# Projecting K and V three tiles ahead of a sequential scan, through a DRAM place per tile

## The chip, the cores and the metric

One core of a Trainium2 chip. The metric is the device time of one execution in microseconds (us). A core has five engines that run their own instruction queues in order and wait for each other by semaphores: TensorE (PE; its weight loads are listed as PEld), VectorE (DVE), ScalarE (ACT), GpSimd (POOL) and SyncE (SP), which only issues DMAs here. ScalarE issues some DMAs too.

## The reference, cut to what matters

```python
k = x @ Wk.T; v = x @ Wv.T          # x: [2, 4096, 512], 16 heads of 32
k = k * cos + rotate_half(k) * sin
def step(W, kc, vc):                # 256 minibatches of 16 tokens, one after the other
    z = kc @ W                      # per batch and head, W starts as the 32x32 unit matrix
    return W - kc.T @ ((z - vc) * 2 / (16 * 32)), z
out = layernorm(zs) * gamma + beta
x = layernorm(x + out @ Wo.T)
h = silu((x @ gate_w.T) * gate_s) * ((x @ up_w.T) * up_s)      # 1408 wide
x = layernorm(x + (h @ down_w.T) * down_s)
```

Only `step` is sequential; K and V of every token depend on x alone.

## The kernel before, in words

The 4096 positions are cut into 32 tiles (NT) of 128 tokens, both batches together. A tile has 8 scan steps (NS). Work is written as **ticks**: tick t, from -1 to 35, has 16 slots, and every engine's program walks the same ticks and slots with its own part. In tick t the kernel projects tile t (n), scans tile t-1 (sc), does the first layernorm, the output projection and the second layernorm of tile t-2 (o), and most of the FFN of tile t-3. The first two FFN blocks of tile o (GATE_UP, DOWN and LOW give slot and block) come in slots 14 and 15.

Projection. x of the tile arrives transposed in x_fm (one buffer, load_x_fm on SyncE); ScalarE makes its high part in fm[0] (high_x, L602), VectorE the low part in fm[1] (low_x, L1076). `project` (L762) does 12 matmuls of 128x512 for one of K and V and one batch; this is called a unit here. K goes to a PSUM bank and from there by `rotate` (L989, three VectorE operations) and `add_rotated` (L481, GpSimd) to k_tok; V by `copy_v` (L583, ScalarE) to v_tok or k_sin. A usual tick has K and V of the second batch of tile t in slots 1 and 4, and those of the first batch of tile t+1 in slots 12 to 14.

K and V then go to DRAM (store_k, store_v; k_scr and v_scr hold one tile) and come back as rows per head (load_rows, 8 DMAs for each half tile of K and of V). K is also needed transposed: for tiles 0 to 2 TensorE transposes it (turn_k, L845), from tile 3 on (EARLY_TICKS) VectorE transposes 32x32 blocks into `turned` and four DMAs and one load turn the rest through kT_scr. z and x1 of tile o take the same way through zT_scr and x1T_scr (store_x1T, L376, load_x1T, L382).

Scan. An even slot has scan_z (L727): z = k W into PSUM. VectorE subtracts v (scan_err, L1012), ScalarE saves z over v_rows (save_z, L558). An odd slot has scan_state (L746), k^T err, and VectorE adds it to the state (step_state, L1022), for which the next scan_z waits. z is stored to z_scr and loaded as tokens (store_z, load_z) in three pieces; VectorE's stats_of begins the layernorm of tile o in slot 0 of the next tick.

Order of the head. The weights gate, up and down are copied DRAM to DRAM and then loaded by ScalarE's queue during ticks -1 to 2 (copy_ffn, load_ffn), and `weigh` (L1086) reduces each piece on VectorE (WEIGHED gives the slots) to find whether the FFN matmuls may run in a faster exact format. TensorE branches on that in tick 2 before slot 14, after GpSimd's all-reduce (L548). In ticks 1 and 2 the projection units are cut in quarters and halves. In the last ticks, 32 has no projection, 33 to 35 no scan.

SyncE's tick (L412) is one list of waits and issues in order: rows of the scanned tile's second half, v store, out store, z turn, x, k and v stores, z store, kT store, first z load, kT load, first-half rows, x1 turn with v rows between its store and its load, x_fm of a later tile, the rest of z.

Of the kernel before, what the change touches and what calls it, by code (L numbers as in the profile page):

```python
# [7 lines left out]
F32 = mybir.dt.float32  # L8
# [41 lines left out]
HALF_UNITS = {1: (0, 2), 2: (2, NC)}  # L50
LAST = NT - 1
LONE = 1
# [17 lines left out]
def build(nc, xT, x, wkT, wvT, woT, gamma, beta, gwT, uwT, dwT, gs, us, ds_row, rope, ident, begin, halves, out):  # L70
    with ExitStack() as ctx:
# [6 lines left out]
        k_scr = nc.dram_tensor("k_scr", [BATCH, P, DM], F32, kind="Internal").ap()  # L78
        v_scr = nc.dram_tensor("v_scr", [BATCH, P, DM], F32, kind="Internal").ap()
        z_scr = nc.dram_tensor("z_scr", [NS, P, 2, P], F32, kind="Internal").ap()  # L80
        kT_scr = nc.dram_tensor("kT_scr", [HQ, HEAD, HQ, NG, HEAD], F32, kind="Internal").ap()
# [31 lines left out]
        v_tok = [sb("v_tok", [P, DM]), k_sin]  # L113
# [18 lines left out]
        hid = [sb(f"hid{i}", [P, TOK]) for i in range(2)]  # L132
# [98 lines left out]
        def v_bank(n, b):  # L231
            return (gu_acc, down_acc[1])[b] if n == 0 else down_acc[0] if n < EARLY_TICKS else work

        def k_by_dma(n):
            return n >= EARLY_TICKS

        def kT_before(n):
            return max(0, n - EARLY_TICKS)

# [31 lines left out]
        def _(sp):  # L271
# [27 lines left out]
            def load_rows(scr, half, b):  # L299

                i0 = half * NS // 2
                for hg in range(NC):
# [4 lines left out]
                                 scr[b, i0 * MB:i0 * MB + P // 2, hg * P:(hg + 1) * P]  # L307
                                 .rearrange("(i t) c -> t i c", t=MB)).then_inc(rows_in[half], 16)

            def load_k_half0(n):  # L310
                sp.wait_ge(k_stored, 16 * (n + 1))
                if n >= 1:
                    sp.wait_ge(state_added, 4 * NS * (n - 1) + 2 * NS)
                for b in range(BATCH):
                    load_rows(k_scr, 0, b)

            def load_v_half0(n, b):
# [4 lines left out]
                load_rows(v_scr, 0, b)  # L322

            def load_k_half1(n):
                if n >= 1:
                    sp.wait_ge(state_added, 4 * NS * n)
                for b in range(BATCH):
                    load_rows(k_scr, 1, b)

            def load_v_half1(n):  # L330
                if n >= 1:
                    sp.wait_ge(z_stored, 48 * n)
                for b in range(BATCH):
                    load_rows(v_scr, 1, b)

            def store_v(n, b):
                sp.wait_ge(v_ready, 2 * n + b + 1)
                if b == 0 and n >= 1:
                    sp.wait_ge(rows_in[0], 256 * n)
                    sp.wait_ge(rows_in[1], 256 * n)  # L340
                sp.dma_start(v_scr[b], v_tok[b][:]).then_inc(v_stored, 16)
# [11 lines left out]
            def store_kT(n):  # L353
                sp.wait_ge(k_turned, 2 * n + 2)
                sp.wait_ge(kT_in, 16 * n)
                store_turned(kT_scr, kT_stored)

            def load_kT(n):
# [3 lines left out]
                             kT_scr.rearrange("h d a g t -> (h d) (a g t)")).then_inc(kT_in, 16)  # L362
# [7 lines left out]
            def load_znT(n):  # L370
                sp.wait_ge(znT_stored, 64 * zT_before(n + 1))
                sp.wait_ge(x1_lo_ready, 2 * n)
                sp.dma_start(landed[:].rearrange("p a g t -> p (a g t)"),
# [14 lines left out]
            def load_x(n):  # L388
                if n == 0:
                    sp.wait_ge(w_low, 2 * NC)  # L390
# [21 lines left out]
            def tick(t):  # L412
                sc, o, y = t - 1, t - 2, t - 4
                if within(sc) and sc >= 1:
                    load_k_half1(sc)
                if within(sc) and sc >= 1:
                    load_v_half1(sc)
                if within(t):
                    store_v(t, 0)
                if y == LAST:  # L420
                    for b in range(BATCH):
                        sp.wait_ge(y_ready, 2 * y + b + 1)
                        sp.dma_start(out[b, rows(y), :], y_tok[:, b, :]).then_inc(out_stored, 16)
                elif within(y):
                    sp.wait_ge(y_ready, 2 * y + 2)
                    sp.dma_start(out[:, rows(y), :].rearrange("b t f -> t b f"), y_tok[:]).then_inc(out_stored, 16)
                if within(o) and z_by_dma(o):
                    store_znT(o)
                    load_znT(o)
                if within(o):  # L430
                    load_x(o)
                if within(t):
                    store_k(t)
                    store_v(t, 1)
                if t == 0:
                    load_k_half0(t)
                    load_k_half1(t)
                if within(sc):
                    store_z(sc, 0, NS // 2)
                if within(t) and k_by_dma(t):  # L440
                    store_kT(t)
                if within(sc):
                    load_z(sc, 0, NS // 2, 16)
                if within(t) and k_by_dma(t):
                    load_kT(t)
                if within(t) and t >= 1:
                    load_k_half0(t)
                if within(o) and z_by_dma(o):
                    store_x1T(o)
                if within(t) and t >= 2:  # L450
                    load_v_half0(t, 0)
                if within(o) and z_by_dma(o):
                    load_x1T(o)
                if within(t) and t >= 2:
# [771 lines left out]
```

## Time and profile before

| | us |
|---|---|
| runs, median of 3 | 1939.27 (1938.07 to 1940.27) |
| profiled execution, device time | 1946.0 |
| its span, first to last instruction | 1944.2 |
| TensorE busy | 1852.8 (95%), 25792 matmuls |
| VectorE busy | 1186.0 (61%) |
| ScalarE busy | 547.9 (28%) |
| GpSimd busy | 638.4 (33%) |
| mean granted TensorE clock | 0.983 |

A busy share is taken over the whole span. The rows further down are of single stretches. A timeline row has start, duration, engine, line, operation, output and inputs, the count of merged instructions and, in brackets, the idle time before it and what ended it. Matmuls overlap in the pipeline, so their price is the distance from start to start. A tick's start is that of the scan_z (L740) of its slot 0.

### The profile page before, as it was taken

What the parts mean: (1) busy time and instruction counts of PE and PEld (TensorE: products, weight loads), DVE (VectorE), ACT (ScalarE), POOL (GpSimd) and SP (SyncE); (2) the same over time, 40 slices, a digit from 0 to 9 for tenths busy, and PEclk for the clock granted to TensorE, in tenths of its full rate; (3) what the DMA queues carried; (4) which work ended last, traced back from release to release, by engine and by line L of the source; (5) the groups of instructions that cost most, each with busy time, mean ns of one, the idle gap of its engine ahead of it and who ended that gap; (6) DMA issues with size and microseconds to landing.
All of it is one profiled execution on the core that took longest, in us unless ns stands there. A gap on an engine that the chain in (4) does not pass through costs nothing.

```text
span 1944.2 us, 60610 instructions
## 1 busy us (share of the span) xinstructions
PE 1852.8 (95%) x25792; PEld 1478.3 (76%) x25792; DVE 1186.0 (61%) x2612; ACT 547.9 (28%) x1236; POOL 638.4 (33%) x775
## 2 busy tenths in 40 slices
PE   6569999999999999999999999999999999999887
PEld 4348777877877777877777787777878878777676
DVE  3555666666666656666665666666666666666643
ACT  2113222232223232322223232222322232322222
POOL 1113333333333333333333333333333333333333
PEclk9779999999999999999999999999999999999999
DMA  7674554455444455545445545444554544555310
GB/s 265 201 222 134 152 151 129 140 166 165 140 147 147 141 146 162 157 144 155 127 144 161 164 143 159 148 130 141 165 167 139 151 147 137 148 153 150 93 55 23
DMA packets 302512, 287.26 MB, mean 148 GB/s; under 512 B 42784, under 2 KB 252320, under 8 KB 302112
## 3 DMA queue, kind: packets, MB, share of 16 engines
q1 hardware_dynamic: 295968, 265.26, 46.0%
q10 hardware_dynamic: 6272, 18.09, 2.7%
q8 instruction: 205, 3.36, 0.7%
q14 instruction: 67, 0.55, 0.1%
HBM read 152.65 MB, written 139.20 MB: 150 GB/s over the span
## 4 chain that ended last, share of the span: by engine, by line
PE 76%; DVE 9%; DMA 7%; SPq 4%; ACT 2%; issue 2%; ACTq 0%; POOL 0%; POOLq 0%; DVEq 0%
PE gu_acc L787 30%; PE work L768 24%; PE down_acc L799 13%; PE scan_acc L740 4%; PE scan_acc L757 3%; DVE x_tok L956 2%; SPq L306 2%; DMA z_scr<-v_rows 2%; DVE hid L1032 2%; DMA landed<-x1T_scr 2%; DVE turned L961 2%; DVE state L1027 1%; DMA landed<-zT_scr 1%; SPq L350 1%; ACT hid L571 1%
## 5 line engine op out<-in xcount | busy, mean ns | idle before, releaser
L500 POOL TENSOR_TENSOR hid_lo<-hid,hid_hi 128x256 fp32r<-128x256 f32 x352 | 263.0, 747 | 629.9 <-ACT hid_hi L581 629.8
L787 PE MATMUL gu_acc<-x_hi,gw 128*128 128x256 f32 x1372 | 375.2, 306 | 8.7 <-DVE hid L1032 3.2
L571 ACT ACTIVATE hid<-gu_acc,gate_scale 128x256 f32<-128x256 f32 x343 | 162.6, 474 | 765.6 <-PE gu_acc L787 765.4
L1032 DVE SCALAR_TENSOR_TENSOR hid<-gu_acc,up_scale,hid 128x256 f32<-128x256 f32 x343 | 165.5, 483 | 300.5 <-ACT hid L571 300.5
L787 PE MATMUL gu_acc<-x_lo,gw 128*128 128x256 f32 x1372 | 339.5, 280 | 0.0
L787 PE MATMUL gu_acc<-x_hi,uw 128*128 128x256 f32 x1372 | 338.8, 280 | 0.0
L787 PE MATMUL gu_acc<-x_lo,uw 128*128 128x256 f32 x1372 | 338.0, 279 | 0.0
L1027 DVE SCALAR_TENSOR_TENSOR state<-scan_acc,half_step,state 128x256 f32<-128x256 f32 x512 | 223.5, 478 | 170.2 <-PE scan_acc L757 164.9
L787 PEld LDWEIGHTS gu_acc<-x_hi,gw 128*128 128x128 f32 x1372 | 258.0, 188 | 44.9 <-DVE hid L1032 18.7
L799 PE MATMUL down_acc<-dw,hid_hi 128*128 128x512 f32 x704 | 282.0, 401 | 2.4 <-POOL hid_lo L500 2.2
L799 PE MATMUL down_acc<-dw,hid_lo 128*128 128x512 f32 x704 | 279.1, 396 | 0.0
L787 PEld LDWEIGHTS gu_acc<-x_lo,gw 128*128 128x128 f32 x1372 | 259.0, 189 | 0.4
L787 PEld LDWEIGHTS gu_acc<-x_hi,uw 128*128 128x128 f32 x1372 | 258.2, 188 | 0.0
L787 PEld LDWEIGHTS gu_acc<-x_lo,uw 128*128 128x128 f32 x1372 | 258.0, 188 | 0.0
L768 PE MATMUL work<-wk,fm 128*128 128x512 f32 x756 | 202.9, 417 | 11.1 <-DVE fm L1078 11.1
L768 PE MATMUL work<-wo,fm 128*128 128x512 f32 x768 | 196.6, 405 | 7.8 <-DVE x_tok L1074 4.5
L581 ACT ACTIVATE hid_hi<-hid 128x256 fp32r<-128x256 f32 x352 | 146.9, 417 | 139.7 <-DVE hid L1032 138.4
L768 PE MATMUL work<-wv,fm 128*128 128x512 f32 x696 | 180.1, 401 | 4.2 <-DVE k_sin L1009 4.2
L560 ACT ACTIVATE v_rows<-scan_acc 128x256 f32<-128x256 f32 x256 | 97.6, 381 | 292.6 <-DVE err L1017 283.2
L768 PEld LDWEIGHTS work<-wk,fm 128*128 128x128 f32 x756 | 141.4, 195 | 47.3 <-DVE fm L1078 11.5
L768 PEld LDWEIGHTS work<-wo,fm 128*128 128x128 f32 x768 | 141.0, 190 | 41.1 <-issue 5.0
L740 PEld LDWEIGHTS scan_acc<-state,k_cols 64*32 64x32 f32 x8192 | 75.9, 107 | 124.2 <-issue 97.8
(121 smaller groups left out, 2230.4 us busy)
## 6 DMA issues: line engine op xcount, KB each, us to landing
x_fm<-xT SPq DMA_DIRECT2D x64, 256.0 KB, 3.4
k_scr<-k_tok SPq DMA_DIRECT2D x32, 512.0 KB, 6.6
k_rows<-k_scr SPq DMA_DIRECT2D x512, 32.0 KB, 2.1
z_scr<-v_rows SPq DMA_DIRECT2D x32, 512.0 KB, 3.5
z_tok<-z_scr SPq DMA_DIRECT2D x512, 32.0 KB, 1.8
x_tok<-x SPq DMA_DIRECT2D x32, 512.0 KB, 5.7
out<-x_tok SPq DMA_DIRECT2D x31, 512.0 KB, 3.4
v_rows<-v_scr SPq DMA_DIRECT2D x488, 32.0 KB, 2.0
```

What stands on the lines that cost most here:

```text
L306: sp.dma_start(place[:, i0:i0 + NS // 2, :], scr[b, i0 * MB:i0 * MB + P // 2, hg * P:(hg + 1) * P] .rearrange("(i t) c -> t i c", t=MB)).t ...
L500: pool.tensor_tensor(hid_lo[m % RING][:], hid[m % 2][:], hid_hi[m % RING][:].bitcast(F32), ALU.subtract).then_inc(hid_lo_ready, 1)
L560: act.activation(v_rows[:, i].rearrange("p a (r c) -> p a r c", r=2), z_acc.rearrange("p r (a c) -> p a r c", a=2), ACT.Copy).then_inc(z_s ...
L571: act.activation(hid[m % 2][:], gu_bank(n, m)[:, 0:TOK], ACT.Silu, scale=gate_scale[:, m:m + 1]).then_inc(silu_done, 1)
L581: act.activation(hid_hi[m % RING][:], hid[m % 2][:], ACT.Copy).then_inc(hid_hi_ready, 1)
L740: mm = pe.matmul(z_acc[j * HEAD:(j + 1) * HEAD, r, odd * 2 * HEAD:(odd + 1) * 2 * HEAD], lhsT=k_cols[k, i // 2, g, i % 2, :], rhs=state[k, ...
L757: mm = pe.matmul(step_acc[q, j, :], lhsT=k_rows[k, i, q], rhs=err[k, :, h, :], start=True, stop=True, skip_group_check=True, tile_position ...
L768: mm = pe.matmul(acc[:], lhsT=fm[p_x][:, c, b, :], rhs=w[p_w][:, c, :], start=(c == 0 and k == 0), stop=(c == NC - 1 and k == 2))
L787: mm = pe.matmul(gu_bank(n, m)[:, k * TOK:(k + 1) * TOK], lhsT=w[:, c, m * P:(m + 1) * P].bitcast(dt), rhs=part[:, c].bitcast(dt), start=( ...
L799: mm = pe.matmul(down_acc[b][:], lhsT=part[m % RING][:, b * P:(b + 1) * P].bitcast(dt), rhs=dw[:, m, :].bitcast(dt), start=(m == 0 and par ...
L1027: dve.scalar_tensor_tensor(part, step_acc.rearrange("p j (o e) -> p j o e", o=2), half_step[:, e:e + 1], part, ALU.mult, ALU.add).then_inc ...
L1032: dve.scalar_tensor_tensor(hid[m % 2][:], gu_bank(n, m)[:, TOK:2 * TOK], up_scale[:, m:m + 1], hid[m % 2][:], ALU.mult, ALU.mult).then_inc ...
```

## The change

K and V of a tile are projected three ticks earlier (LEAD): in a usual tick t the units are those of tile t+3, and of t+4 in slots 12 to 14. k_scr, v_scr and kT_scr get one place per tile, so that stores wait for no load. Tick 1 has a half unit in each of its 16 slots (8 units) and four whole units behind slot 15; tick 2 has six units in slots 0 to 5 and two more in halves in slots 9, 10, 12 and 13. Ticks 29 to 31 have no units left, tick 28 none in slots 12 to 14. Staging for odd tiles up to 5 is lent by v_tok, hid and landed, for even ones v uses x_tok. K of tiles 0 and 1 is transposed on TensorE, from tile 2 on by DMA. In ticks 1 and 2 low_x is on GpSimd, the scaling of wo on ScalarE, and the FFN weights are copied, loaded and weighed in other slots; v rows of tile 1 are loaded by SyncE.

```diff
-WEIGHED = {(1, 13): (0,), (1, 15): (1,), (2, 1): (2,), (2, 3): (3,), (2, 6): (4,), (2, 8): (5,), (2, 10): (6,), (2, 11): (7,),
-           (2, 12): (8,), (2, 13): (9, 10, 11)}
-EARLY_TICKS = 3
+WEIGHED = {(1, 5): (0,), (1, 8): (1,), (1, 11): (2,), (1, 13): (3,), (2, 0): (4,), (2, 2): (5,), (2, 4): (6,), (2, 6): (7,),
+           (2, 9): (8,), (2, 10): (9,), (2, 11): (10,), (2, 13): (11,)}
+STEADY = 3
+LEAD = 3
+FRONT = STEADY + LEAD
+BY_PE = 2
+HALVES = ((0, 2), (2, NC))
+FIRST_UNITS = ((K, 1, 1), (V, 1, 1), (K, 2, 0), (V, 2, 0), (K, 2, 1), (V, 2, 1), (K, 3, 0), (V, 3, 0))
+MIDDLE_UNITS = ((K, 3, 1), (V, 3, 1), (K, 4, 0), (V, 4, 0))
+SECOND_UNITS = ((K, 4, 1), (V, 4, 1), (K, 5, 0), (V, 5, 0), (K, 5, 1), (V, 5, 1))
...
-        k_scr = nc.dram_tensor("k_scr", [BATCH, P, DM], F32, kind="Internal").ap()
+        k_scr = nc.dram_tensor("k_scr", [NT, BATCH, P, DM], F32, kind="Internal").ap()
...
+        def k_half(n, b):
+            if n < FRONT and n % 2:
+                return v_tok[:] if b == 0 else hid_both[:].rearrange("p a t -> p (a t)")
+            return k_tok[:, b, :]
+        def v_half(n, b):
+            if n == 0 or n >= FRONT:
+                return (v_tok, k_sin)[b][:]
+            if n % 2:
+                return landed[:].rearrange("p h g t -> p (h g t)")[:, b * DM:(b + 1) * DM]
+            return x_tok[:, b, :]
...
             def store_k(n):
-                sp.wait_ge(k_ready, 2 * n + 2)
-                sp.dma_start(k_scr.rearrange("b t f -> t b f"), k_tok[:]).then_inc(k_stored, 16)
+                sp.wait_ge(k_stored, 32 * n)
+                for b in range(BATCH):
+                    sp.wait_ge(k_ready, 2 * n + b + 1)
+                    sp.dma_start(k_scr[n, b], k_half(n, b)).then_inc(k_stored, 16)
...
             def load_x(n):
                 if n == 0:
-                    sp.wait_ge(w_low, 2 * NC)
+                    sp.wait_ge(v_stored, 32 * (FRONT - 1))
...
+                elif t == 1:
+                    store_v(1, 0)
+                    store_k(1)
+                    store_v(1, 1)
+                    load_x_fm(3)
+                    store_z(0, 0, NS // 2)
+                    load_k_half0(1)
+                    load_z(0, 0, NS // 2, 16)
+                    store_v(2, 0)
+                    load_v_half0(1, 0)
+                    load_v_half0(1, 1)
+                    store_k(2)
+                    store_z(0, NS // 2, NS - 1)
+                    store_v(2, 1)
+                    load_x_fm(4)
+                    load_z(0, NS // 2, NS - 1, 32)
+                    store_kT(2)
+                    store_z(0, NS - 1, NS)
+                    load_z(0, NS - 1, NS, 48)
+                elif t == 2:
+                    load_k_half1(1)
+                    load_v_half1(1)
+                    store_v(3, 0)
+                    store_k(3)
+                    store_v(3, 1)
+                    load_x_fm(5)
+                    store_v(4, 0)
+                    store_kT(3)
+                    store_k(4)
+                    store_v(4, 1)
+                    load_kT(2)
+                    load_x_fm(6)
+                    load_x(0)
+                    store_v(5, 0)
+                    store_kT(4)
+                    store_k(5)
+                    store_z(1, 0, NS // 2)
+                    store_v(5, 1)
+                    load_k_half0(2)
+                    load_z(1, 0, NS // 2, 16)
+                    store_kT(5)
+                    load_v_half0(2, 0)
+                    load_v_half0(2, 1)
+                    load_x_fm(7)
...
+                else:
...
+                    if within(n):
+                        store_v(n, 0)
...
+                    if within(t):
+                        load_kT(t)
+                        load_k_half0(t)
...
+            def low_x(n, b):
+                pool.wait_ge(x_high, 2 * n + b + 1)
+                pool.tensor_tensor(fm[1][:, :, b, :], x_fm[:, :, b, :], fm[0][:, :, b, :].bitcast(F32),
+                                   ALU.subtract).then_inc(x_low, 1)
...
-                if within(o + 2):
-                    pe.wait_ge(v_ready, 2 * (o + 2) + 2)
+                if o == 0:
+                    pe.wait_ge(k_mul, 6 * FRONT)
+                elif within(o + 2 + LEAD):
+                    pe.wait_ge(v_ready, 2 * (o + 2 + LEAD) + 2)
...
+                    if t == 1:
+                        unit(*FIRST_UNITS[s // 2], *HALVES[s % 2])
+                    if t == 1 and s == 15:
+                        for middle in MIDDLE_UNITS:
+                            unit(*middle, 0, NC)
+                    if t == 2 and s < len(SECOND_UNITS):
+                        unit(*SECOND_UNITS[s], 0, NC)
+                    if t >= STEADY and within(n) and s == 1:
+                        project_k(n, 1, 0, NC)
+                    if t >= STEADY and within(n) and s == 4:
+                        project_v(n, 1, 0, NC)
...
+                    if t == 2 and s in (9, 10):
+                        project_k(FRONT, 0, *HALVES[s - 9])
+                    if t == 2 and s in (12, 13):
+                        project_v(FRONT, 0, *HALVES[s - 12])
...
-                    if within(o) and s == (0 if o != LAST else 3):
+                    if within(o) and s == (2 if o == 0 else 3 if o == LAST else 0):
                         dve.wait_ge(z_tok_in, 256 * (o + 1))
                         stats_of(0, 0, z_tok)
```

## Rows read from the trace of the kernel before

**Rows 1.** Windows: busy time per engine in stretches: ticks 1, 2, a usual one, 31, 32.

```profile
core 0: us, PE busy (x) PEld busy (x) DVE busy (x) ACT busy (x) POOL busy (x), PEclk, DMA share, GB/s
34.30:73.40 39.10, 26.89 (x573) 15.83 (x572) 20.40 (x42) 8.24 (x18) 4.17 (x7) 0.83 0.72 231
73.40:150.10 76.70, 43.63 (x645) 31.89 (x644) 39.42 (x68) 11.66 (x23) 9.16 (x12) 0.76 0.63 199
1523.90:1580.90 57.00, 56.80 (x805) 45.51 (x804) 36.46 (x82) 16.77 (x38) 20.14 (x25) 1.00 0.50 150
1752.90:1808.80 55.90, 52.51 (x781) 42.31 (x780) 33.92 (x77) 15.24 (x35) 19.20 (x24) 0.97 0.49 143
1808.80:1861.50 52.70, 45.96 (x758) 36.89 (x757) 31.50 (x72) 14.68 (x35) 16.71 (x21) 1.00 0.33 99
```

**Rows 2.** Timeline of TensorE, ticks 1 and 2: the large gaps.

```profile
70.13 0.47 PE L757 MATMUL scan_acc<-err,k_rows 32*32 32x64 f32 x16 [4.33 <-ACT v_rows L560]
...
90.25 0.68 PE L740 MATMUL scan_acc<-state,k_cols 64*32 64x64 f32 x32 [9.96 <-DVE state L1027]
...
112.55 5.37 PE L768 MATMUL work<-wo,fm 128*128 128x512 f32 x12 [3.54 <-DVE x_tok L1074]
...
141.38 0.68 PE L740 MATMUL scan_acc<-state,k_cols 64*32 64x64 f32 x32 [7.53 <-issue]
```

**Rows 3.** Waits of the head, and what VectorE and GpSimd do before the branch.

```profile
ACT v_rows L560 <- issue: 9.5, 1, 9.5
DVE stats L942 <- DMA z_tok<-z_scr: 11.1, 1, 11.1
...
132.05 1.74 DVE L1089 TENSOR_REDUCE low_half<-dw 128x1 f32<-128x1536 uint16 x1
...
132.21 1.29 POOL L484 TENSOR_TENSOR k_tok<-k_tok,k_sin 128x512 f32<-128x512 f32 x1 [10.60 <-DVE k_sin L1009]
...
139.65 0.17 DVE L1182 TENSOR_REDUCE low_half<-low_half 128x1 f32<-128x12 f32 x1
```

**Rows 4.** Timeline of TensorE: one unit in a usual tick, and what follows it.

```profile
1527.68 3.06 PE L768 MATMUL work<-wk,fm 128*128 128x512 f32 x12
1530.67 0.45 PE L740 MATMUL scan_acc<-state,k_cols 64*32 64x64 f32 x32
```

**Rows 5.** Timeline of TensorE, ticks 31 and 32: slot 12, and a gap of each.

```profile
1795.38 0.45 PE L740 MATMUL scan_acc<-state,k_cols 64*32 64x64 f32 x32
...
1800.90 0.68 PE L740 MATMUL scan_acc<-state,k_cols 64*32 64x64 f32 x32 [2.49 <-DVE state L1027]
...
1814.89 0.46 PE L740 MATMUL scan_acc<-state,k_cols 64*32 64x64 f32 x32 [2.28 <-DVE state L1027]
...
1850.49 0.46 PE L740 MATMUL scan_acc<-state,k_cols 64*32 64x64 f32 x32
```

**Rows 6.** Timeline of SyncE: the x1 turn in tick 31 and in tick 32.

```profile
1789.61 1.75 SPq L350 DMA_DIRECT2D x1T_scr<-turned  x4
...
1794.84 0.34 SPq L385 DMA_DIRECT2D landed<-x1T_scr  x1
...
1844.72 1.76 SPq L350 DMA_DIRECT2D x1T_scr<-turned  x4
...
1848.38 0.34 SPq L385 DMA_DIRECT2D landed<-x1T_scr  x1
```

**Rows 7.** DMA of 34.3 to 150.1: bytes, queues' share of 16 engines, us to landing.

```profile
DMA packets 19338, 24.25 MB, mean 209 GB/s; under 512 B 2652, under 2 KB 14142, under 8 KB 19262
...
q10 hardware_dynamic: 5539, 14.96, 38.8%
q1 hardware_dynamic: 13787, 9.12, 26.8%
...
x_fm<-xT SPq DMA_DIRECT2D x6, 256.0 KB, 3.7
...
k_scr<-k_tok SPq DMA_DIRECT2D x2, 512.0 KB, 7.4
```

More of the change, by code:

```diff
@@ L130, in build @@
         x1_lo = sb("x1_lo", [P, NC, BATCH, P], F32R)
-        hid = [sb(f"hid{i}", [P, TOK]) for i in range(2)]
+        hid_both = sb("hid", [P, 2, TOK])
+        hid = [hid_both[:, i, :] for i in range(2)]
         hid_hi = [sb(f"hid_hi{i}", [P, TOK], F32R) for i in range(RING)]
@@ L412, in tick @@
             def tick(t):
[L413 to L454, printed above, removed]
-                    load_v_half0(t, 1)
@@ L691, in tick @@
                             copy_ffn(0, c)
-                    if within(t) and not k_by_dma(t) and s == (9 if t == LONE else 6):
+                    if within(t) and not k_by_dma(t) and s == (7 if t == 1 else 6):
                         copy_kT(t, 0)
@@ L698, in tick @@
                         act.wait_ge(small_in, 16 * SMALL)
+                    if t == 1 and s in (1, 3, 5, 7):
+                        scale_wo(s // 2)
                     if t == 1 and s in (2, 4, 6, 8):
@@ L1124, in tick @@
                         normalize(1, o, 1, x1_tok[o % 2], x_tok, x1_ready)
-                    if within(t + 1) and s == 11:
+                    if t <= 0 and s == 11:
                         low_x(t + 1, 1)
+                    if t >= STEADY - 1 and within(n + 1) and s == 11:
+                        low_x(n + 1, 1)
                     if within(o) and s == (12 if o != LAST else 10):
@@ L1146, in tick @@
                         moments_of(0, o)
-                    if within(o) and s == (1 if o != LAST else 4):
+                    if within(o) and s == (3 if o == 0 else 4 if o == LAST else 1):
                         normalize(0, o, 0, z_tok, z_tok, zn_ready)
@@ L1156, in tick @@
                         turn_x1(o, 1)
-                    if within(t) and s == (5 if t == LONE else 2):
-                        rotate(t, 1)
-                    if within(o) and s == (5 if o != LAST else 6):
+                    if t == 0 and s == 2:
+                        rotate(0, 1)
+                    if t >= STEADY and within(n) and s == 2:
+                        rotate(n, 1)
+                    if within(o) and s == (6 if o in (0, LAST) else 5):
                         low_zn(o, 1)
-                    if within(t + 1) and s == 7:
+                    if t <= 0 and s == 7:
                         low_x(t + 1, 0)
+                    if t == 2 and s == 8:
+                        low_x(FRONT, 0)
+                    if t >= STEADY and within(n + 1) and s == 7:
+                        low_x(n + 1, 0)
                     if t == -1 and s == 12:
```

449 lines of the change are left out of this document (314 added, 135 removed).

## The prediction, made before the changed kernel was seen to run

> **What bounds the kernel now.** I read the stretches first [rows 1]. In a usual tick (1523.9 to 1580.9) TensorE is busy 56.80 of 57.00 us at the full clock, so nothing but its own work sets the tick. Three places are different. Ticks 1 and 2 last 39.1 and 76.7 us and hold 26.9 and 43.6 us of TensorE work, part of it at half clock (granted 0.83 and 0.76). Tick 31 (55.9 us) lacks the first batch's projections of a next tile, and tick 32 (52.7 us) has none. So the kernel has room at the head and loses cover at the tail; the change moves TensorE work from the tail ticks to the head.
>
> Then the TensorE rows of the head [rows 2]. A TensorE row in brackets is a gap with its releaser. Tick 1 runs from 34.3 to 73.4, tick 2 to 150.1. Large gaps: 4.33 us before 70.13 (ScalarE saved z late: it stood 9.5 us in its own issues [rows 3], the eight row loads of load_v_rows among them), 9.96 before 90.25, 3.54 before 112.55, 7.53 before 141.38. The 9.96 is VectorE standing 11.1 us for z_tok's DMA [rows 3], with step_state behind it in the same queue. The 7.53 is the end of weigh: the last reduction ends at 139.8, GpSimd's all-reduce follows, then TensorE branches [rows 3]. A scan step's two matmul groups are priced at 0.7 us together below, their rows of 0.45 and 0.47 [rows 2, 4] less the overlap.
>
> Last the TensorE rows of ticks 31 and 32, and SyncE's for the x1 turn [rows 5, 6].
>
> **The size of what moves.** One unit (12 matmuls, one of K/V, one batch) takes 1530.67 - 1527.68 = 2.99 us from start to start [rows 4]; four per tile. After the change ticks 1 and 2 hold 20 units (8 + 4 middle, then 6 + 2) instead of 8: 12 more, 12 x 2.99 = 35.9 us. They leave tick 28 (two), ticks 29 and 30 (four each) and tick 31 (two). The time changes only by what the head stretches and the tail shrinks.
>
> **The tail.** Tick 32 already is a tick with scan and FFN and no unit. It lost 4 x 2.99 = 12.0 us of work against a usual tick but only 57.0 - 52.7 = 4.3 us of time [rows 1]: TensorE idles 52.7 - 46.0 = 6.7 us in it, the longest gap 2.28 us, for state [rows 5]. These are scan latencies that the units had covered, and the next thing late is step_state behind other VectorE work. By halves: slots 0 to 11 take 1850.5 - 1808.8 = 41.7 us against 1795.4 - 1752.9 = 42.5 in tick 31, which has its two units there: 0.8 back of 6.0. Slots 12 to 15 take 1861.5 - 1850.5 = 11.0, against 1808.8 - 1795.4 = 13.4 in tick 31 and 57.0 - 42.5 = 14.5 in a usual one.
> The two ends of slots 12 to 15 differ through one wait. In tick 31 SyncE issues the x1T load 5.23 us after its stores began, in tick 32 3.66 [rows 6]; four v_rows loads of the next tile stand between. With the load late, ScalarE's x_hi and VectorE's x_lo are late, step_state waits behind x_lo, TensorE idles 2.49 us.
> Worst: all four shortened ticks end in 13.4: tick 28 gives 1.1, 29 and 30 give 57.0 - 55.1 = 1.9 each, 31 gives 55.9 - 55.1 = 0.8; together 5.7 us. Best: all end in 11.0: 3.5 + 4.3 + 4.3 + 3.2 = 15.3 us. Four stores issue in 1.75 us, so four loads as quick would be through after 3.5 and fit before the 3.66 at which tick 32 issues: the 5.23 of tick 31 is more than its queue explains, and I stand nearer to tick 32: 10 us gained. In ticks 29 to 31 SyncE also loses store_k, store_v, store_kT and x_fm; no queue gets anything more.
>
> **The usual ticks, 3 to 27.** TensorE's order is the same. store_k becomes two DMAs (one more issue on SyncE), kT and rows are loaded for a tile stored three ticks before, so load_kT and the k and v row loads wait for no landing. The rotate and copy waits keep their form, shifted. All of it lies under 56.8 of 57.0 us of TensorE work: 0. If that cover were gone, the extra issue would cost some 0.4 us a tick (one issue takes 0.34 to 0.44 [rows 6]), 10 us in all. Bounds: the 25 ticks have 0.2 us of idle each [rows 1], so at most 5 us to win, more likely none, and a hiccup in two or three of them to lose: -3 to +3 us.
>
> **The head.** Tick 1: a scan step with a half unit after each part is 0.7 + 2 x 1.5 = 3.7 us of TensorE work. Before, with quarter units, the tick took 39.1 us, 4.33 of them that gap: 34.8 us or 4.3 a step, more than TensorE's work: latency of err, save and state. I take 35 us again, then four middle units, 12 us, of which none covers a scan; start of tick 2 at 34 + 47 = 81 to 82, against 73.4. The wait for ScalarE's issue (4.33) and most of the 9.96 go: load_v_rows(1) moves to SyncE, and stats of z_tok move from slot 0 to 2, behind two to four units.
> What the units need: x_fm has one buffer. Tile n+1 is loaded only when both low halves of tile n are made, lands 3.7 us later [rows 7] or more, then ScalarE and GpSimd do one 128x512 operation each, 1.3 us each at most (GpSimd's add [rows 3]); that is up to 6.3 us after low_x(n, 1), and units K and V of (n, 1) fill 6.0. Just enough, if SyncE comes to it in time and the DMA is quick. The queue ahead on SyncE in tick 2 is 16 row loads (16 x 0.44 = 7 us), two v stores and k: I allow 3 us of stalls in tick 2.
> Also moved: low_x of tiles 2 to 5 goes from VectorE to GpSimd, 8 x 1.3 = 10 us on an engine busy 13.3 of 115.8 us [rows 1]; scale_wo goes from VectorE to ScalarE (19.9 us busy in 115.8 [rows 1]); both free VectorE and lie beside TensorE's units.
> Tick 2: slots 0 to 5, 3 x (0.7 + 6.0) = 20 us; 3 of stalls; two project_o with their turn and the wait for add_o (x is loaded only after v of tile 4 is stored, because x_tok is its staging; it was 3.5 us late before and stays so), 10 us; slots 8 to 13 with two units in halves, turn_x1, four weigh of up to 1.74 us [rows 3] and K rotation on VectorE, 20 us; slots 14 and 15 as before, 150.1 - 141.4 = 8.7. Sum 62, against 76.7. Tick 3 begins at 82 + 62 = 144 to 145; before 150.1. Gain 5 us.
> Bounds. DMA: in this stretch 24.25 MB took 66% of 16 engines for 115.8 us, that is 316 GB/s when busy [rows 7]. The change adds three tiles each of x, k and v, four kT stores and one kT load, 14 x 0.524 = 7.3 MB. 31.6 MB at 316 GB/s are 100 us: best, a gain of 16. At tick 1's mean, 231 GB/s [rows 1], 137 us: a loss of 21.
> The page "DMA: Bandwidth & Descriptors" (Bandwidth) of the Trainium skill gives about 358 GB/s as a core's HBM limit; by it the bytes alone would take an estimated 88 us. No run here shows that rate over such a stretch, and the sum does not use it.
>
> **Sum.** Profiled execution 1946.0 us: -5 (head), 0, -10 (tail) = 1931.0. It lies 6.7 us above the median of the runs, 1939.27; so 1924.3.
>
> **Rivals.**
> (a) The head fills without stalls, as fast as the bytes allow, and the tail ends well: -16 - 13 = -29, 1910 us. For: TensorE had 45 us free there. Against: k lands after a median of 7.4 us in the head [rows 7], and x_fm may come to that too. Chance 0.12.
> (b) The head eats the tail's gain: FFN copies, row loads and three more tiles share 16 DMA engines, and SyncE serves x_fm behind waits for k_ready and for landing z. Head +8 to +13: within 0.2%. Chance 0.10.
> (c) The same at 231 GB/s: +21 - 10 = +11, 1950 us. It decides from the point where ticks 1 and 2 together pass 126 us. For: the bytes grow by 30%, and the queue is one and in order. Against: the DMA engines idle a third of the time now. Chance 0.10.
> (d) TensorE's clock. The thinned ticks 28 to 32 have gaps; after the 2.49 us gap of tick 31 the granted clock is 0.97 over it, and in the head, with gaps, 0.76 to 0.83 [rows 1]. If ticks 29 to 32 ran at the head's 0.76, 46 us of work would take 60 and each tick some 8 us more than my 53.5: +32 - 15 = +17, 1956 us. Against: tick 32 itself has 6 us of gaps and granted 1.00. Chance 0.03. The page "TensorE: Matmul & The Clock Gate" (HAM oscillation) says that bursts shorter than the waits between them let the clock fall before each burst, so that each begins at half. By this case's rows that holds in the head and not in tick 32, whose bursts are longer than its gaps.
> (e) That it doesn't do what it says can be left out: units, places and waits are written out in the diff.
>
> **How the numbers follow.** Forecast 0.65, (a) 0.12, (b) 0.10, (c) 0.10, (d) 0.03. A measurement here can tell about 0.2%, 3.9 us. Faster: 0.77, same 0.10, slower 0.13. The forecast alone spans head -12 to +2, tail -15 to -6 and up to 3 from the usual ticks, 1909 to 1935; the range with the inner parts of (a), (b) and the near end of (c) is 1908 to 1941.
>
> **What would show it.** Tick 2 begins near 82 and tick 3 near 145; the 4.33 and 9.96 gaps are gone, the 7.53 is smaller; DMA share of the head is over 0.8. Usual ticks stay 57.0. Ticks 29 to 31 take 52.7 to 55.1, with gaps before z, err and project_o as in tick 32. Wrong if tick 3 begins after 160, if x_fm or z_tok is what TensorE or VectorE waits for there by over 10 us, or if ticks 29 to 31 run at half clock.

## The result, and the profile after

| | before | after |
|---|---|---|
| median of the runs, us | 1938.67 (1934.59 to 1940.27) | 1956.11 (1949.63 to 1958.09) |
| ratio, 95% interval | | 1.0087 (1.0062 to 1.0111) |
| profiled execution, us | 1946.0 | 1949.63 |
| its span, us | 1944.2 | 1947.5 |
| TensorE busy, us | 1852.8 | 1856.3 |

The change makes the kernel slower by 17 us; the forecast was 15 us faster. The profiled execution is the shortest of the changed kernel's four. Windows of the changed kernel, cut at its tick starts: ticks 1, 2, 3, then 28 to 31. They stand beside [rows 1].

```profile
core 0: us, PE busy (x) PEld busy (x) DVE busy (x) ACT busy (x) POOL busy (x), PEclk, DMA share, GB/s
33.40:92.40 59.00, 48.63 (x665) 34.04 (x664) 29.22 (x52) 15.62 (x30) 17.06 (x17) 0.91 0.89 293
92.40:165.50 73.10, 51.84 (x689) 38.74 (x688) 41.85 (x77) 12.76 (x25) 15.02 (x17) 0.81 0.63 197
165.50:222.50 57.00, 56.59 (x804) 45.34 (x804) 35.41 (x79) 16.69 (x38) 19.47 (x23) 1.00 0.48 140
1594.20:1650.40 56.20, 52.93 (x786) 42.67 (x786) 33.83 (x77) 15.36 (x35) 19.14 (x24) 0.97 0.49 143
1650.40:1705.40 55.00, 48.48 (x757) 39.55 (x756) 31.34 (x72) 14.63 (x34) 17.23 (x23) 0.94 0.39 116
1705.40:1759.10 53.70, 45.96 (x758) 36.94 (x757) 31.25 (x72) 14.64 (x34) 17.43 (x23) 1.00 0.39 117
1759.10:1814.20 55.10, 48.85 (x761) 39.94 (x761) 31.11 (x72) 14.75 (x34) 17.48 (x23) 0.94 0.40 119
```

The head is the loss: tick 3 begins at 165.5, not at 144.5 (before: 150.1). The usual ticks are as they were: ticks 3 to 27 take 1428.7 us, before 1430.8. The tail gains: ticks 28 to 31 take 220.0 us against 227.9 for ticks 28 to 31 before. Note the 0.94 in ticks 29 and 31, and that tick 30 at 1.00 is the shortest.

TensorE's timeline of the changed kernel's head, the large gaps:

```profile
84.19 5.49 PE L955 MATMUL work<-wk,fm 128*128 128x512 f32 x12 [6.63 <-POOL fm L560]
...
108.82 5.16 PE L955 MATMUL work<-wk,fm 128*128 128x512 f32 x12 [9.26 <-POOL fm L560]
...
130.53 4.58 PE L955 MATMUL work<-wo,fm 128*128 128x512 f32 x12 [2.00 <-DVE x_tok L1281]
...
155.22 0.68 PE L927 MATMUL scan_acc<-state,k_cols 64*32 64x64 f32 x32 [3.01 <-issue]
```

The 4.33 and 9.96 of [rows 2] are gone and the 7.53 became 3.01, as forecast. In their place stand two new ones, before K of tile 4 and before K of tile 5: GpSimd's low part of x is not there. The waits of ticks 1 and 2 give the next link, ScalarE, and what it waits for:

```profile
engine line waited for: us in total, times, longest us
POOL fm L560 <- ACT fm L730: 45.6, 6, 14.7
...
ACT fm L730 <- DMA x_fm<-xT: 26.5, 4, 12.8
```

So it is x_fm's DMA. SyncE's timeline says why that is late:

```profile
69.44 3.86 SPq L325 DMA_DIRECT2D v_rows<-v_scr  x8
73.40 0.86 SPq L365 DMA_DIRECT2D k_scr<-k_tok  x2
...
75.59 2.14 SPq L295 DMA_DIRECT2D x_fm<-xT  x2
...
84.14 0.73 SPq L307 DMA_DIRECT2D z_scr<-v_rows  x1
90.55 0.77 SPq L316 DMA_DIRECT2D z_tok<-z_scr  x2
91.36 3.71 SPq L325 DMA_DIRECT2D k_rows<-k_scr  x8
95.11 5.12 SPq L325 DMA_DIRECT2D v_rows<-v_scr  x8
...
102.22 1.36 SPq L295 DMA_DIRECT2D x_fm<-xT  x2
```

x_fm was free for tile 4 at 67.1 (low_x(3, 1) ends) and its load is issued at 75.59, 8.5 us late, behind row loads and stores. It was free for tile 5 at 86.6 and the load is issued at 102.22, 15.6 us late: SyncE stands from 84.9 to 90.5 for the landing of a z store, then issues 16 row loads in 9 us, then four stores. From the issue, tile 4's x takes 6.6 us and tile 5's 4.6 us until ScalarE can begin, and 2.0 us more until K's matmuls start. And the loads take longer to land. The DMA view of 33.4 to 165.5, against [rows 7]:

```profile
DMA packets 27084, 31.70 MB, mean 240 GB/s; under 512 B 3661, under 2 KB 20221, under 8 KB 27005
...
x_fm<-xT SPq DMA_DIRECT2D x12, 256.0 KB, 5.1
```

The bytes are the 31.6 MB forecast; x_fm lands after a median of 5.1 us, before 3.7; in the second profile of each kernel it is 4.3 against 3.9. The page "DMA: Bandwidth & Descriptors" (Latency and other measured facts) of the Trainium skill says that HBM's access latency grows under load; the trace agrees in kind, at a DMA share of 0.89 in tick 1 (before: 0.72), but it does not tell latency of the memory from time spent behind other transfers.

Last, the tail. TensorE's timeline around the start of tick 29 in the changed kernel, and a window behind the second gap:

```profile
1641.98 0.46 PE L927 MATMUL scan_acc<-state,k_cols 64*32 64x64 f32 x32 [2.24 <-DVE state L1234]
...
1656.44 0.68 PE L927 MATMUL scan_acc<-state,k_cols 64*32 64x64 f32 x32 [2.28 <-DVE state L1234]
```

```profile
core 0: us, PE busy (x) PEld busy (x) DVE busy (x) ACT busy (x) POOL busy (x), PEclk, DMA share, GB/s
1656.30:1659.70 3.40, 3.25 (x44) 3.09 (x45) 3.37 (x8) 0.00 (x0) 0.97 (x3) 0.50 0.12 42
```

Each thinned tick has such gaps near slots 1 and 13, and most of them are followed by a stretch at 0.50, 1.2 GHz. From tick 28 to 1830 these add up to 20 us at half clock, in the kernel before to 3.4 us. They vary from execution to execution: again, the second profile of the changed kernel, has 34 us there, and before_again, a second one of the kernel before, 6.8.

### The profile page after: what moved, and what is told of

It reads as the page before. It is cut to its first block, busy times and chain, and to the rows that moved or that the text cites. A ratio compares the mean times of both kernels' runs of the same rounds, so it can differ in the third digit from the quotient of the medians.

```text
span 1947.5 us, 60662 instructions
## 1 busy us (share of the span) xinstructions
PE 1856.3 (95%) x25784; PEld 1483.4 (76%) x25784; DVE 1182.8 (61%) x2602; ACT 550.9 (28%) x1238; POOL 653.3 (34%) x783
## 3 DMA queue, kind: packets, MB, share of 16 engines
q8 instruction: 204, 3.34, 0.7%
## 4 chain that ended last, share of the span: by engine, by line
PE 78%; DVE 10%; DMA 5%; SPq 3%; ACT 2%; issue 1%; ACTq 0%; POOL 0%; POOLq 0%; DVEq 0%
PE gu_acc L974 32%; PE work L955 24%; PE down_acc L988 13%; PE scan_acc L927 4%; PE scan_acc L944 4%; DMA landed<-x1T_scr 2%; DVE x_tok L1154 2%; DVE state L1234 2%; DVE hid L1239 2%; DVE turned L1159 2%; SPq L325 1%; SPq L370 1%; DMA z_scr<-v_rows 1%; ACT hid L687 1%; PE scan_acc L974 1%
## 5 line engine op out<-in xcount | busy, mean ns | idle before, releaser
L974 PE MATMUL gu_acc<-x_hi,gw 128*128 128x256 f32 x1372 | 379.5, 309 | 11.5 <-DVE hid L1239 5.5
L974 PE MATMUL gu_acc<-x_lo,gw 128*128 128x256 f32 x1372 | 343.6, 283 | 0.0
L697 ACT ACTIVATE hid_hi<-hid 128x256 fp32r<-128x256 f32 x352 | 146.9, 417 | 138.9 <-DVE hid L1239 137.1
L955 PE MATMUL work<-wv,fm 128*128 128x512 f32 x624 | 162.5, 403 | 2.3 <-DVE k_sin L1216 2.0
L927 PEld LDWEIGHTS scan_acc<-state,k_cols 64*32 64x32 f32 x8192 | 75.7, 107 | 116.4 <-issue 92.1
```

The lines of the kernel that those rows point to most:

```text
L697: act.activation(hid_hi[m % RING][:], hid[m % 2], ACT.Copy).then_inc(hid_hi_ready, 1)
L927: mm = pe.matmul(z_acc[j * HEAD:(j + 1) * HEAD, r, odd * 2 * HEAD:(odd + 1) * 2 * HEAD], lhsT=k_cols[k, i // 2, g, i % 2, :], rhs=state[k, ...
L955: mm = pe.matmul(acc[:], lhsT=fm[p_x][:, c, b, :], rhs=w[p_w][:, c, :], start=(c == 0 and k == 0), stop=(c == NC - 1 and k == 2))
L974: mm = pe.matmul(gu_bank(n, m)[:, k * TOK:(k + 1) * TOK], lhsT=w[:, c, m * P:(m + 1) * P].bitcast(dt), rhs=part[:, c].bitcast(dt), start=( ...
```

## The experiments

Ratios are to the kernel before in the same job, with their 95% interval; 0.1% is 1.9 us. Where only the profiled execution is named, it is one execution.

**Again.** The changed kernel, unedited.

> The changed kernel once more, unedited, beside the others of this job; its further profile also tells what differs between executions. Both theories: 1950 to 1958 us, tick 2 begins near 92, tick 3 near 165 us, TensorE waits twice for the low half of x (6 to 9 us each) in front of K of tile 4 and K of tile 5.

1955.37 us, 1.0078 (1.0050 to 1.0105); profiled 1955.37, tick 3 at 167.7. The loss repeats, as expected. The average of the two ratios, 1.0082, is what the edits below are read against.

**The queue.** x_early issues x_fm of tiles 4 and 5 earlier on SyncE:

```diff
                     store_v(2, 0)
+                    load_x_fm(4)
                     load_v_half0(1, 0)
...
                     store_v(2, 1)
-                    load_x_fm(4)
...
                     store_z(0, NS - 1, NS)
+                    load_x_fm(5)
                     load_z(0, NS - 1, NS, 48)
...
                     store_v(3, 1)
-                    load_x_fm(5)
```

> Theory Q (SyncE's order): the loads of x_fm for tiles 4 and 5 were issued 8.5 and 15.6 us after their low halves were free, behind row loads, stores and the landing of z. Issued ahead of these, both TensorE gaps (6.6 and 9.3 us) go, tick 3 begins at 146 to 151 and the time falls by 13 to 19 us, to about 1939. Theory D (bytes): 16 DMA engines are 0.89 busy in tick 1, so an earlier issue lands later and delays the rest; tick 3 begins at 160 or later, the time falls by less than 5 us.

1949.70 us, 1.0051 (1.0031 to 1.0071); tick 3 at 157.1. TensorE's gaps in the head of x_early:

```profile
80.28 4.62 PE L955 MATMUL work<-wk,fm 128*128 128x512 f32 x12 [2.54 <-POOL fm L560]
...
106.06 5.46 PE L955 MATMUL work<-wk,fm 128*128 128x512 f32 x12 [4.60 <-DVE k_sin L1216]
```

That lies between the two theories: tick 3 is 10.7 us earlier than the average of the changed head (below), the time falls by about 6 us. 6.63 became 2.54, and where 9.26 stood the releaser is another: VectorE's rotation of K of tile 5. Its output goes to the place from which store_k(3) still reads, and SyncE's timeline of x_early has that store behind the row loads:

```profile
90.46 3.97 SPq L325 DMA_DIRECT2D k_rows<-k_scr  x8
94.47 4.71 SPq L325 DMA_DIRECT2D v_rows<-v_scr  x8
99.28 0.37 SPq L359 DMA_DIRECT2D v_scr<-landed  x1
...
100.18 0.56 SPq L365 DMA_DIRECT2D k_scr<-hid  x1
```

So queue2 also takes the stores of tile 3 ahead of those 16 loads:

```diff
-                    load_x_fm(5)
+                    store_v(3, 0)
+                    load_x_fm(5)
+                    store_k(3)
+                    store_v(3, 1)
                     load_z(0, NS - 1, NS, 48)
                 elif t == 2:
                     load_k_half1(1)
                     load_v_half1(1)
-                    store_v(3, 0)
-                    store_k(3)
-                    store_v(3, 1)
```

> As x_early, and SyncE also stores k and v of tile 3 before the 16 row loads of tick 2, since rotate of tile 5 waited for that store there (gap of 4.6 us in x_early). Theory Q: that gap goes and tick 3 begins 4 to 6 us earlier than the 157.1 of x_early, at 151 to 153: no earlier than before the change (150.2), because four units behind slot 15 (12 us) lie beside no scan step. Time 3 to 6 us under x_early's. If the bytes bound it, the gap moves to another load and tick 3 stays at 156 or later.

1944.71 us, 1.0031 (1.0018 to 1.0044); tick 3 at 155.5. The order of one queue is worth 0.5%, 10 us, with the same instructions and bytes. The time fell as forecast, but tick 3 did not come at 151 to 153. One gap is left in tick 2 of queue2, 4.89 us for the same GpSimd row: x_fm of tile 5, free at 84.0 and issued at 88.38 here, still comes behind a z store, and it lands only after 8.6 us.

**The bytes.** thin leaves out 9 of the 12 copies of the FFN weights from DRAM to DRAM; all pieces are loaded from the first one's place, so the weights in the FFN are not the reference's.

```diff
             def copy_ffn(i, c):
+                if c > 0:
+                    return
...
-                act.wait_ge(ffn_copied[i][c], 16)
-                act.dma_start(dst[:, c0:c1].bitcast(F32), src[c0 * P:c1 * P].rearrange("(c p) n -> p c n", p=P)
+                act.wait_ge(ffn_copied[i][0], 16)
+                act.dma_start(dst[:, c0:c1].bitcast(F32), src[0:(c1 - c0) * P].rearrange("(c p) n -> p c n", p=P)
```

> Of gate, up and down only the first piece is copied in DRAM and every piece is loaded from it, so 9 of 12 copies (6.3 MB) are left out and the FFN's weights are other ones. Theory Q: x_fm of tile 5 still stands behind 16 row loads and two landings; at most a third of the gaps goes, the time falls by 2 to 7 us. Theory D: with 20% fewer bytes in ticks 1 and 2 the gaps go, the time falls by 12 us or more.

1947.50 us, 1.0039 (1.0021 to 1.0057); tick 3 at 156.2. Windows of ticks 1 and 2 of thin, its bytes over both, and its largest gap:

```profile
core 0: us, PE busy (x) PEld busy (x) DVE busy (x) ACT busy (x) POOL busy (x), PEclk, DMA share, GB/s
34.40:83.40 49.00, 44.38 (x665) 31.12 (x664) 29.03 (x52) 15.40 (x30) 17.10 (x16) 1.00 0.87 273
83.40:156.20 72.80, 51.61 (x685) 38.59 (x684) 41.74 (x77) 12.63 (x25) 15.05 (x17) 0.81 0.63 191
```

```profile
DMA packets 25428, 27.24 MB, mean 224 GB/s; under 512 B 3470, under 2 KB 19637, under 8 KB 25397
```

```profile
99.86 5.03 PE L957 MATMUL work<-wk,fm 128*128 128x512 f32 x12 [9.28 <-POOL fm L560]
```

With 4.5 MB less (14%, not the 20% expected), the time again falls between the two theories. Tick 1 is 10 us shorter, and part of that is the clock, 1.00 in place of 0.91: the gap of 6.63 is 2.13 there. Tick 2 is as long as with the bytes, and the gap for tile 5 is the same 9.28: here its load was issued 13.1 us after x_fm was free, so that one is the queue's. queue2_thin has both edits:

> queue2 with 9 of the 12 DRAM copies of the FFN weights left out (the FFN's weights are other ones), for theory D with the queue out of the way. If bytes now hold the rest of the head, landings fall from 5 to 8 us to 3 to 5 us, tick 3 begins at 148 or earlier and the time is 6 us or more under queue2's 1944.7. If not, tick 3 stays at 152 to 155.

1938.81 us, 0.9987 (0.9971 to 1.0004); tick 3 at 148.9. The copies' bytes are worth 0.43 to 0.44%, 8 us, with either order. Even so tick 3 begins no earlier than before the change. The landings did not fall as expected: x_fm of tile 5 still takes 8.7 us, with a gap of 4.61 us behind it. Two things stay open. thin also takes the copies' issues, some 0.5 us each, off ScalarE's queue; and no run leaves the copies out of the kernel before, so the 8 us are what these bytes are worth in the changed head, not shown to be what the change's own 7.3 MB cost.

**A shorter lead.** lead2 projects two tiles ahead: 16 units in ticks 1 and 2, no middle units, one tile less of x, k and v in the head.

```diff
-LEAD = 3
+LEAD = 2
...
-MIDDLE_UNITS = ((K, 3, 1), (V, 3, 1), (K, 4, 0), (V, 4, 0))
-SECOND_UNITS = ((K, 4, 1), (V, 4, 1), (K, 5, 0), (V, 5, 0), (K, 5, 1), (V, 5, 1))
+SECOND_UNITS = ((K, 3, 1), (V, 3, 1), (K, 4, 0), (V, 4, 0), (K, 4, 1), (V, 4, 1))
...
-                    if within(o) and s == 4:
+                    if within(o) and s == (6 if o == 0 else 4):
                         add_bias(o, 0)
```

> K and V two tiles ahead instead of three: no units behind slot 15 of tick 1, tick 2 has the units of tiles 3 and 4, x_fm of tile 4 is loaded early. Theory Q with the cover argument: the head sheds 12 us of TensorE work that no scan step covered and both gaps, tick 3 begins at 133 to 140; the tail has three thinned ticks instead of four and gives 2 to 3 us less. 1925 to 1935 us, faster than before the change. Theory D: tick 3 begins at 150 or later.

1952.75 us, 1.0072 (1.0045 to 1.0099); tick 2 at 75.7, tick 3 at 171.9. TensorE's gaps in tick 2 of lead2:

```profile
85.04 0.79 PE L928 MATMUL scan_acc<-err,k_rows 32*32 32x64 f32 x32 [5.90 <-DVE err L1205]
...
106.33 0.68 PE L911 MATMUL scan_acc<-state,k_cols 64*32 64x64 f32 x32 [9.38 <-DVE state L1215]
...
135.30 5.23 PE L939 MATMUL work<-wo,fm 128*128 128x512 f32 x12 [14.40 <-DVE x_tok L1262]
```

A miss. Tick 2 takes 96.2 us. The middle units had covered z's round trip through DRAM; without them step_state stands behind z_tok again, as before the change (9.96 in [rows 2]). The 14.40 is x: x_tok is the staging of V of tile 4, now projected late, and x is loaded at 129.10. This run moves the wait and does not price the lead itself.

**The x1 turn.** tail_x1 lets no row load stand between the x1T stores and the load, from tick 28 on.

```diff
-                    if within(t):
+                    if within(t) and t < NT - LEAD - 1:
                         load_v_half0(t, 0)
                     if within(o) and z_by_dma(o):
                         load_x1T(o)
+                    if within(t) and t >= NT - LEAD - 1:
+                        load_v_half0(t, 0)
```

> From tick 28 on SyncE issues the x1T load ahead of all eight v row loads instead of behind four. If the gap of 1.8 to 2.6 us near slot 13 in ticks 28 to 31 is the late x1T load, it becomes the 0.6 to 1.0 of tick 32 and each of the four ticks is 1.3 to 2.4 us shorter, with the half-clock stretch after it gone: 6 to 8 us in all. If it is VectorE's own order, nothing changes (within 2 us).

1952.18 us, 1.0067 (1.0045 to 1.0089): not told apart from the changed kernel. SyncE's timeline of tick 29, in tail_x1:

```profile
1690.57 3.29 SPq L370 DMA_DIRECT2D x1T_scr<-turned  x4
1695.64 0.34 SPq L406 DMA_DIRECT2D landed<-x1T_scr  x1
```

5.07 us, with four loads less between; the changed kernel has 5.24 there (1686.00 and 1691.24). In tail_x1 nothing is issued between the end of the stores' issue (1693.86) and the load, and a store of this turn lands after a median of 3.0 us. The load waits for the stores to land, not for its place in the queue.

**The clock.** warm fills the short gaps of the thinned ticks with work that nobody reads: eight matmuls of 128x512 before the waits in slots 1 and 13 of ticks 28 to 32 (28: slot 13 alone).

```diff
+            def keep_warm(o):
+                pe.wait_ge(o_added, 2 * o)
+                for i in range(2 * NC):
+                    pe.matmul(work[:], lhsT=wo[0][:, i // 2, 0:P], rhs=wk[0][:, i // 2, :], start=(i == 0), stop=(i == 2 * NC - 1))
...
+                    if NT - LEAD <= t <= NT and s == 1:
+                        keep_warm(o)
+                    if NT - LEAD - 1 <= t <= NT and s == 13:
+                        keep_warm(o + 1)
```

> Eight extra matmuls of 128x512 into a free bank (1.7 us) in slots 1 and 13 of ticks 28 to 32, where TensorE idled 2.3 to 2.6 us; their result is not used. Theory C (clock): these gaps bring the half-clock stretches of the thinned ticks (31 to 50 us in the tail against 16 before the change), and a stretch costs half its length. With the gaps filled the half-clock time from tick 28 on falls to 16 us or less and the time by 5 to 12 us although work was added; runs differ less from each other. If the gaps themselves are the whole price, the time stays within 2 us or rises.

1946.74 us, 1.0046 (1.0025 to 1.0066). Windows of ticks 29 to 31 of warm:

```profile
core 0: us, PE busy (x) PEld busy (x) DVE busy (x) ACT busy (x) POOL busy (x), PEclk, DMA share, GB/s
1650.00:1702.70 52.70, 49.91 (x778) 39.88 (x778) 30.43 (x72) 14.65 (x34) 17.05 (x23) 1.00 0.41 122
1702.70:1754.90 52.20, 49.79 (x776) 39.84 (x776) 31.24 (x72) 14.64 (x34) 17.42 (x23) 1.00 0.41 122
1754.90:1807.00 52.10, 49.75 (x776) 39.85 (x776) 30.35 (x72) 14.65 (x34) 17.17 (x23) 1.00 0.41 124
```

Here TensorE does more work and the ticks are shorter: 157.0 us in all, 163.8 in the changed kernel. The longest gap from 1590 to 1810 is 0.76 us and no stretch there runs at half clock. The starts of scan_z give the price of one stretch: from slot 2 to slot 4 a step takes 6.99 us in all three ticks of warm and in tick 30 of the changed kernel, and 8.15 and 8.25 in its ticks 29 and 31, which have half clock there; from slot 14 to the next tick 6.79 to 6.86 against 8.06 and 8.38. That is 1.2 to 1.5 us for each stretch, and six stretches of the changed kernel's tail 7 to 9 us. Tick 30 has none; its 53.7 against 52.2 lies in slots 6 and 7, where the output projection waited 1.73 us for the low part of z, whose turn through zT_scr landed late. The run's ratio says 0.36%, 7 us. The same fill in the kernel before (ticks 31 and 32 alone) is before_warm, the control:

> The kernel before the change, with the eight extra matmuls in slot 13 of tick 31 and slots 1 and 13 of tick 32, where it too idles. It tells how much of warm's gain the kernel before could have had as well. Theory C: it has two thinned ticks instead of five and 16 us at half clock in its tail, so 1 to 4 us under the kernel before, against the 9 us that warm gained.

1939.40 us, 0.9991 (0.9974 to 1.0009): not told apart from nothing, though the interval does not exclude the 1 to 4 us expected, and from tick 28 to the end its profile has 359.8 us against 362.8 in three profiles without the fill. Most of the loss to the clock belongs to the thinned ticks that the change adds. lead2 with the fill:

> lead2 with the extra matmuls of warm (in its thinned ticks). Theory C: 3 to 8 us under lead2, 1920 to 1930 us. Otherwise within 2 us of lead2 or above it.

1948.40 us, 1.0052 (1.0032 to 1.0072), 0.2% from lead2, within the intervals of both. Its one profile agrees with theory C all the same: from tick 28 to the end it takes 352.1 us, lead2's 358.6.

**Queue and clock together.** queue2_warm is queue2 with the fill of warm.

> Both repairs at once. If the two causes are separate, their gains of 11 us (queue2) and 9 us (warm) add up: 1935 to 1937 us, 2 to 4 us under the kernel before the change; tick 3 begins at 155, ticks 28 to 31 take 52 to 55 us each, half clock in the tail about 10 us. If they share a cause, 1940 us or more.

1936.96 us, 0.9979 (0.9963 to 0.9995): this one is faster than both kernels, by 4 us against the one before. Against before_warm, the kernel before with the same fill, it is 2.4 us, which the intervals do not tell from nothing. Tick 3 begins at 161.6 here, not at the 155 expected, with queue2's order of the head: from one execution to the next this head moves by 6 us. The two profiles average 158.5, 9 us ahead of the changed kernel's. queue3_warm issues x_fm(5) ahead of kT and of the last z store too:

```diff
+                    load_x_fm(5)
                     store_kT(2)
                     store_z(0, NS - 1, NS)
                     store_v(3, 0)
-                    load_x_fm(5)
                     store_k(3)
```

> As queue2_warm, and x_fm of tile 5 is issued before the stores of kT and of the last z piece, about 3 us earlier. Theory Q: the gap of 4.9 us before K of tile 5 shrinks to about 2 and the time falls by 2 to 3 us, to 1932 to 1935 us. If its slow landing (6.8 to 8.1 us against a median of 3.5 in the whole run) is what counts, less than 1.5 us.

1938.26 us, 0.9992 (0.9976 to 1.0009); not told apart from queue2_warm. x_fm of tile 5 was issued 2.9 us after it was free and no gap of TensorE above 2 us waits for it any more, but others have grown: the output projection waits 5.61 us for x_tok, in queue2_warm 3.34. Moving this load further ahead gave nothing more.

**The kernel before, again.** before_again and before_third are the kernel before, unedited, for where its tick 3 begins.

> The kernel before the change, unedited. Its first profile has tick 3 at 150.2 us in an execution of 1946.0, 7 us above its median. If its head varies with the landings of the weights and of z, tick 3 begins at 143 to 147 in an execution near 1939 and the ticks from 3 on take the same; then the change cost the head about 20 us, not 15. If the 7 us lie elsewhere, tick 3 stays at 150.

> The same once more, for the spread of its head and its tail from execution to execution: tick 3 between 143 and 151, ticks 28 to 31 within 226 to 228 us together.

before_again: 1943.01 us, 1.0010 (0.9993 to 1.0027), its own scatter; before_third: one execution, 1944.65. Ticks 28 to 31 take 226.6 and 227.4 us. Tick 3 begins at 147.0 and 146.2. With before_warm's 144.3 the four profiles of this head average 146.9, and the 150.2 of [rows 2] is the latest of them. The four profiles with the changed head (the changed kernel, again, tail_x1, warm) have 165.5, 167.7, 170.0 and 167.9, on average 167.8. The head costs 20.9 us, not the 15.4 that the two first profiles show.

## Why the prediction was wrong, point by point

**Where the forecast failed** is one term: "I allow 3 us of stalls in tick 2", and with it the clause "Just enough, if SyncE comes to it in time and the DMA is quick". Neither held. The chain from low_x(n, 1) to the next unit was costed at 6.3 us with x_fm's load issued at once; it was issued 8.5 and 15.6 us late. I had counted 16 row loads, two v stores and k as 7 us of queue, but not as a delay that x_fm sees in full, nor the wait for the landing z store ahead of them, and had allowed no stall for tile 4, in the middle units, at all. Measured from the end of low_x(n, 1) to K's first matmul, the chain took 17.1 us for tile 4 (8.5 until the issue, 6.6 until ScalarE began, 2.0 of preparation) and 22.2 us for tile 5 (15.6, 4.6 and 2.0). By stages: slots 0 to 15 of tick 1 took 38.4 us (forecast 35), the middle units 20.6 (12), slots 0 to 5 of tick 2 32.4 (23 with the stalls), the rest 40.7 (38.7). Two of the four terms miss by 8.6 and 9.4 us, and they hold the two gaps of 6.63 and 9.26, each with a stretch at half clock behind it (a unit of 5.49 and 5.16 us in place of 3.06). The other two miss by 3.4 and 2.0, which no run takes apart.

**The sum** has the head at +20.9 us by four profiles each, ticks 3 to 27 at 1428.5 against 1431.1 (-2.6), and from tick 28 to the end 355.1 (two profiles) against 362.8 (three): -7.7. That is +10.6, of the 15 to 17 us between the medians. The other 5 or 6 stay open: unprofiled executions of the kernel before are on average some 5 us shorter than its three profiled ones, and those of the changed kernel are not.

**The usual ticks**: 0 forecast, -2.6 measured, within the bounds. **The tail**: 10 us gained forecast, about 8 measured, so right in size, but in part by luck, for its reading was off. "The 5.23 of tick 31 is more than its queue explains" was a misreading: I gave the four loads the 1.75 us of four stores, and the trace of the kernel before has 3.12 for them, so that the issues fill the 5.23 but for 0.4:

```profile
1791.47 3.12 SPq L306 DMA_DIRECT2D v_rows<-v_scr  x4
```

Yet I let the x1 turn decide between the ends, and tail_x1 shows that it does not hang on the loads between: without them the landing of the stores takes as long. What kept the gain down is the clock, as warm shows: with the fill the same stretch takes 344.9 us, 10 less than without.

**Rival (c)**, given 0.10, is the one whose sign came: ticks 1 and 2 took 132.1 us together, past its point of 126, and the head's +21 is its price. Its reason is only a part of it. A mean rate is a result of how full the queue is kept: 240 GB/s with all the bytes, 224 with 4.5 MB less, and in tick 1 of x_early, below, 317 over 53 us, as high as the 316 that the prediction took as its best.

```profile
34.60:87.60 53.00, 46.28 (x665) 32.42 (x664) 29.23 (x52) 15.50 (x30) 17.06 (x17) 0.97 0.94 317
```

The runs give the order of the queue 10 us and the bytes of nine copies 8; what the change's own bytes cost is not shown apart.

**Rival (d)**, given 0.03, was too lightly set aside. That its 1956 us is the median measured is luck: it reached it by 32 us of clock in the tail. I priced it as whole ticks at 0.76 and argued against it that tick 32 has gaps and granted 1.00. It comes as short stretches behind single gaps of 2.2 to 2.6 us, at 0.94 to 0.97 for a tick, and costs 7 us, 10 from queue2. The tick 31 of [rows 1] already had it: one gap of 2.49 us and 0.97. The page "TensorE: Matmul & The Clock Gate" (HAM oscillation) of the Trainium skill has the clock fall over waits longer than the bursts between them; here it falls over waits far shorter than the bursts too: 2.24 us before 1641.98 and 2.28 before 1656.44, with 12 us of work between the two.

**The parts together.** Queue 0.5%, bytes 0.4% and clock 0.4% are 1.3% by three single edits, against a loss of 0.8%: without all three the change would give about 0.5%, 9 us, by this estimate. Part of that may not be the change's: a kernel before without the copies was not run, and leaving them out is no repair. All three together were not run either; two pairs were, and they add up within the intervals (queue2_warm 0.9979 against 0.9995 by the sum, queue2_thin 0.9987 against 0.9988). The forecast's idea, units moved beside an idle engine, was lost to what feeds them and to the clock of what they leave behind.

## What to carry to other kernels

When work is moved into a stage to fill an idle engine, write out the in-order queue that feeds it, issue by issue, and ask of each load when its buffer comes free and what is issued or waited for in between; with one buffer, a late issue becomes the engine's gap as soon as the work in hand is used up. Price bytes and landing time at the load of the fuller stage, not at the average of the emptier one. And work that is taken away to shorten a stage leaves gaps: a gap of two microseconds cost 1.2 to 1.5 more in clock here, so look at the granted clock of the stage that already looks as the others will.

## What the runs showed of the hardware

Eight unused matmuls, twice a tick, make a tick shorter: 16 of them add 3.8 us of busy time (49.8 against 45.96 in tick 30 of the changed kernel, which is at full clock too), all of it inside the gaps, and ticks 29 to 31 shrink by 6.8 us together, most of it because the clock stays at 2.4 GHz. In the kernel before the same gaps, two in ticks 31 and 32, cost nothing that the ratio can tell. Whether a given gap is followed by a half-clock stretch is not fixed: the 2.28 us gap early in tick 32 of the kernel before kept 1.00 in [rows 1], and the same tick of before_again, its last row below, has 0.93.

```profile
1749.20:1805.00 55.80, 52.77 (x788) 42.49 (x791) 32.94 (x77) 15.22 (x35) 18.71 (x24) 0.97 0.48 144
1805.00:1857.50 52.50, 46.61 (x745) 38.06 (x745) 29.59 (x66) 14.14 (x33) 15.79 (x20) 0.93 0.33 99
```

That tick took 52.5 us all the same, 52.7 before. The clock's price is in it: from slot 2 to slot 4 its step takes 8.07 us, in the kernel before 6.99. It is made up in slots 6 and 7, 9.11 us against 10.06, where the length varies between profiles at either clock. So one tick's time does not show what its clock cost; the same step in two profiles does.
